# One VectorE program reordered: cross reciprocal in slot 11, gate denominator behind the keys' last part, slots made in slots 5 to 7

## The reference

```python
x = layernorm(x + attention(x, Wq, Wk, Wv))            # 16 query heads of 16, one shared key and value head
x = layernorm(x + cross_attention(x, context, mask))   # 120 context rows, two projections, a mask added
x = layernorm(x + experts(x, Wg, W1, b1, Wo, bo))      # 8 experts, the top 2 of the gate's softmax
```

## Time and profile before

| | |
|---|---|
| median of three runs | 1377.48 us |
| the profiled execution, its own time | 1376.5 us |
| its span, first to last instruction | 1374.5 us |
| TensorE busy over the span | 1267.1 us (92%) |
| VectorE busy | 1100.1 us (80%) |
| ScalarE busy | 743.4 us (54%) |
| GpSimd busy | 639.8 us (47%) |
| TensorE's granted clock, mean | 0.972 |
| one full step of the first stage | 21.2 us (kstack at 478.29 us and at 499.49 us) |
| draining steps 33 to 38 | from 733 to 805 us |

### The profile page before, as it was taken

How to read it: one execution, slowest core, us unless ns; L and a number is a source line. 1 busy time by engine, 2 the same in 40 slices (tenths; PEclk the granted TensorE clock), 3 DMA queues, 4 the chain that set the end, 5 groups by cost and what they waited for, 6 DMA issues and landing times.

```text
span 1374.5 us, 30245 instructions
## 1 busy us (share of the span) xinstructions
PE 1267.1 (92%) x7734; PEld 895.6 (65%) x7735; DVE 1100.1 (80%) x3115; ACT 743.4 (54%) x1740; POOL 639.8 (47%) x917
## 2 busy tenths in 40 slices
PE   6898999999999999999998659999999999987997
PEld 4444555556556565555654447788888888867997
DVE  0566898898988889989897657788887888876997
ACT  1235777787877788878886313232232322323555
POOL 3011345545554545554554523685555555651333
PEclk9999999999999999999999859999999999998999
DMA  7747588797887978867565775898888888877885
GB/s 187 183 100 143 107 219 202 209 227 189 220 195 189 205 196 216 177 184 162 137 145 187 275 281 89 142 151 134 125 136 133 132 133 128 137 119 233 280 280 178
DMA packets 194871, 242.73 MB, mean 177 GB/s; under 512 B 21712, under 2 KB 144592, under 8 KB 190544
## 3 DMA queue, kind: packets, MB, share of 16 engines
q1 hardware_dynamic: 159392, 153.70, 46.0%
q0 software_dynamic: 26128, 54.94, 23.3%
q10 hardware_dynamic: 9248, 32.86, 7.0%
HBM read 142.46 MB, written 120.24 MB: 191 GB/s over the span
## 4 chain that ended last, share of the span: by engine, by line
PE 70%; DVE 10%; DMA 8%; issue 6%; SPq 2%; POOL 2%; ACT 1%; ACTq 0%; POOLq 0%; DVEq 0%
PE psHb L1441 7%; PE psHb L1438 7%; PE psHb L1437 7%; PE psS L729 5%; PE psO L644 5%; PE psHa L1438 5%; PE psHa L1437 5%; PE psHa L1441 5%; PE psB L673 4%; PE psT L739 4%; DVE negmax L1070 4%; DMA qstack<-q_parts 3%; PE psX L1461 2%; PE psHa L1494 2%; DMA xt<-in_x_t 2%
## 5 line engine op out<-in xcount | busy, mean ns | idle before, releaser
L1070 DVE TENSOR_REDUCE negmax<-psS 128x2 f32<-128x512 f32 x512 | 346.7, 684 | 85.8 <-PE psS L729 84.7
L904 ACT ACTIVATE probs<-psT 128x512 f32<-128x512 f32 x512 | 299.6, 599 | 139.8 <-PE psT L739 127.1
L1518 ACT ACTIVATE hb<-hb 128x512 f32<-128x512 f32 x135 | 85.4, 632 | 285.9 <-DVE hb L1593 248.3
L1402 POOL DMA_INDIRECT g_rows<-g,slot x135 | 212.9, 1577 | 35.9 <-issue 32.9
L729 PE MATMUL psS<-kstack,qstack 96*128 96x256 bf16 x1024 | 194.7, 272 | 31.1 <-DMA qstack<-q_parts 12.6
L739 PE MATMUL psT<-qstack,kstack 99*128 99x512 bf16 x512 | 193.6, 381 | 4.6 <-ACT probs L904 4.4
L729 PEld LDWEIGHTS psS<-kstack,qstack 96*128 96x128 bf16 x1024 | 89.9, 101 | 102.7 <-DVE negmax L1070 30.8
L503 POOL DMA_INDIRECT lists<-x,slots x128 | 128.4, 1003 | 33.9 <-issue 30.1
L644 PE MATMUL psO<-probs,vaug 128*32 128x512 f32 x1024 | 138.8, 615 | 0.4 <-ACT probs L904 0.4
L1602 DVE SCALAR_TENSOR_TENSOR g<-g,xe,hb 128x512 f32<-128x512 f32 x135 | 101.6, 752 | 24.8 <-ACT hb L1518 11.3
L1593 DVE TENSOR_TENSOR hb<-psHb,b 128x512 f32<-128x512 f32 x135 | 93.2, 690 | 31.1 <-issue 27.8
(11 more groups left out here) (210 smaller groups left out, 2792.2 us busy)
## 6 DMA issues: line engine op xcount, KB each, us to landing
qstack<-q_parts SPq DMA_DIRECT2D x192, 128.0 KB
g_rows<-zero_rows ACTq DMA_DIRECT2D x20, 1024.0 KB, 6.6
xe<-lists SPq DMA_DIRECT2D x135, 132.5 KB
rows<-g_rows SPq DMA_DIRECT2D x32, 512.0 KB, 4.5
q_parts<-qpart SPq DMA_DIRECT2D x32, 384.0 KB
sums<-x SPq DMA_DIRECT2D x32, 264.0 KB
x2in<-sums SPq DMA_DIRECT2D x32, 264.0 KB, 3.4
xt<-in_x_t SPq DMA_DIRECT2D x32, 256.0 KB
```

Source lines behind the costliest of these rows:

```text
L904: nc.scalar.activation(probs[:, u % PT, :], psT[:, u % 2, :], ACT.Exp, scale=SELF_SCALE).then_inc(sm["exp_done"], 1)
L1070: v.tensor_reduce(negmax[:, b1.s2, 2 * hp:2 * hp + 2, c], psS[:, u % 2, :].rearrange("p (h k) -> p h k", h=2), AX.X, ALU.max, negate=True) ...
L1402: pool.indirect_dma_start(out=dram["g_rows"], out_offset=bass.IndirectOffsetOnAxis(ap=slot[:, o.s8:o.s8 + 1], axis=0), in_=g[:, o.s8], in_ ...
```

## The change

The instructions are the same; their places in the in-order programs differ.

- chosen, slotf and slots of batch b7 move from slots 0, 1, 2 to slots 5, 6, 7 of the same step.
- GpSimd no longer waits for slots_ready between the two parts of the queries; it waits ahead of the first dispatch, in every step.
- crec moves from slot 13 to slot 11.
- The gate's denominator moves: its first operation from slot 12 to slot 14, behind the keys' last part; its second from slot 13 to slot 15; its reciprocal from slot 14 to behind slot 15, ahead of L1192, which needs it.

```diff
--- before.py
+++ after.py
@@ -518,7 +518,6 @@
                 pool.tensor_tensor(qpart[:, t.s2, 1], qrest[:, t.s2], one_c[:, :].unsqueeze(2).to_broadcast([P, DC, S]),
                                    ALU.mult).then_inc(sm["q_split"], 1)
 
-                wait(pool, "slots_ready", done(b7))
                 wait(pool, "q_split", 2 * t.n + 1)
                 pool.tensor_tensor(qpart[:, t.s2, 2], qrest[:, t.s2], qpart[:, t.s2, 1], ALU.subtract
                                    ).then_inc(sm["q_split"], 1)
@@ -526,8 +525,7 @@
                 expert_constants()
             if active(b7):
 
-                if not active(t):
-                    wait(pool, "slots_ready", done(b7))
+                wait(pool, "slots_ready", done(b7))
                 dispatch(b7, 0)
             if active(b4):
                 wait(pool, "att_normed", done(b4, 2))
@@ -1073,19 +1071,19 @@
                 if u == 0 and active(b6):
                     wait(dve, "y2_ready", done(b6))
                     stats(y2, stats2, b6, "stats2_ready")
-                if u == 0 and active(b7):
+                if u == 5 and active(b7):
                     wait(dve, "slot_link", 3 * b7.n + 1)
                     v.tensor_tensor(chosen[:, b7.s2], hot[:, b7.s2],
                                     place[:, b7.s2].unsqueeze(2).to_broadcast([P, QC, 2, E]), ALU.mult
                                     ).then_inc(sm["slot_link"], 1)
                 if u == 1 and active(b6):
                     moments(stats2, mv2, b6, "var2_ready")
-                if u == 1 and active(b7):
+                if u == 6 and active(b7):
                     wait(dve, "slot_link", 3 * b7.n + 2)
                     v.tensor_reduce(slotf[:, b7.s2], chosen[:, b7.s2], AX.X, ALU.add).then_inc(sm["slot_link"], 1)
                 if 1 <= u <= 4 and active(b2):
                     split_max(b2, u - 1)
-                if u == 2 and active(b7):
+                if u == 7 and active(b7):
                     wait(dve, "slot_link", 3 * b7.n + 3)
                     v.tensor_copy(slots[:, b7.s2], slotf[:, b7.s2].rearrange("p c k -> p (c k)")
                                   ).then_inc(sm["slots_ready"], 1)
@@ -1147,14 +1145,9 @@
                 if u == 12 and active(b4) and not draining(t):
                     wait(dve, "y1_ready", done(b4))
                     stats(y1, stats1, b4, "stats1_ready")
-                if u == 12 and active(b6):
-
-                    wait(dve, "gate_exp", done(b6))
-                    v.scalar_tensor_tensor(gden[:, b6.s2], gsum[:, b6.s2], GATE_EPS, gtop[:, b6.s2, :, 0], ALU.mult,
-                                           ALU.add).then_inc(sm["gate_link"], 1)
                 if u == 13 and active(b4) and not draining(t):
                     moments(stats1, mv1, b4, "var1_ready")
-                if u == 13 and active(b6):
+                if u == 15 and active(b6):
                     gate(5)
                     v.tensor_tensor(gden[:, b6.s2], gden[:, b6.s2], gtop[:, b6.s2, :, 1], ALU.add
                                     ).then_inc(sm["gate_link"], 1)
@@ -1162,12 +1155,14 @@
                     wait(dve, "k_mid", done(t))
                     v.tensor_tensor(kstack[64:80, t.s4], krest[64:80, t.s2], ksmall[64:80, t.s2], ALU.subtract
                                     ).then_inc(sm["k_split"], 1)
-                if u == 13 and active(b5):
+                if u == 11 and active(b5):
                     wait(dve, "cross_exp", done(b5))
                     v.reciprocal(crec[:, b5.s2], csum[:, b5.s2]).then_inc(sm["crec_ready"], 1)
                 if u == 14 and active(b6):
-                    gate(6)
-                    v.reciprocal(gden[:, b6.s2], gden[:, b6.s2]).then_inc(sm["gate_link"], 1)
+
+                    wait(dve, "gate_exp", done(b6))
+                    v.scalar_tensor_tensor(gden[:, b6.s2], gsum[:, b6.s2], GATE_EPS, gtop[:, b6.s2, :, 0], ALU.mult,
+                                           ALU.add).then_inc(sm["gate_link"], 1)
                 if u == 14 and active(b5):
                     wait(dve, "crec_ready", done(b5))
                     wait(dve, "cross_out", done(b5))
@@ -1186,6 +1181,8 @@
                 copy_keybias(g, part)
             if active(b6):
 
+                gate(6)
+                v.reciprocal(gden[:, b6.s2], gden[:, b6.s2]).then_inc(sm["gate_link"], 1)
                 gate(7)
                 wait(dve, "hot_ready", done(b6))
                 for c in range(QC):
```

## The result

The changed kernel takes 1383.93 us in the median of 13 runs (1378.82 to 1389.15), the kernel before 1377.48 us on the same chip: ratio 1.0048, interval 1.0033 to 1.0063. The profiled execution spans 1380.4 us, 5.9 us more than before's.

| stretch | before | after | |
|---|---|---|---|
| start to the maxima of step 9, slot 0 | 220.49 | 219.60 | -0.9 |
| 23 full steps, from there to step 32, slot 0 | 493.87 | 491.57 | -2.3 |
| to the last slots | 90.54 | 100.44 | +9.9 |
| from there to the experts' first transposes | 14.58 | 13.18 | -1.4 |
| the experts | 555.07 | 555.63 | +0.6 |

The account below looks back on a forecast made before the run. Bound by TensorE-VectorE handoffs in full steps and a chain of waits in draining steps. 0 + 1.7 + 0.5 + 5.8 = 8.0 us slower, 1385.5 us against the median; 8-in-10 range 1377 to 1393 us.

Parts of the forecast that it names:

- Slot 14, taken at 0: Full steps: moving the gate's denominator and crec brings no earlier kstack; 0 us a step, bounds 0 and -0.15.
- second rival: Full steps: VectorE, not TensorE, sets slot 14, so 19 of 24 steps start 0.15 us sooner; 1382.5 us, chance 0.1.
- The tail, 0.4 us: Behind slot 15 of a full step: linked gate operations ahead of L1192 make base 0.4 us later.
- price of 0.07 us a step: Queries' projection waiting for the later base: 0.07 us in each of 25 steps, bounds 0 and 0.25; 1.7 us.
- The dispatches, "I take +0.1" in "5 of 24 steps": Full steps: later dispatches among qstack's loads cost 0.1 us where the load comes last; 0.5 us in all.
- the forecast's own sign of being wrong: Full steps: qstack's load coming last in most steps, where 4 to 6 of 19 were expected.
- first rival: Full steps: the moved dispatches hold up the loads of qstack, 11 us in place of 0.5; 1396 us, chance 0.15.
- "The loss ends in slot 8, where VectorE waits over 1 us for TensorE": Full steps: the 0.25 us that chosen, slotf and slots add in slots 5 to 7 is absorbed by slot 8's wait.
- The draining steps, 5.8 us: Steps 33 to 38: 1.9 us for 33 and 34, 3.6 for 35, 0.3 for 36 to 38; bounds 3 to 8.
- The stall for y1: Step 33, slot 8: VectorE's statistics wait 2.65 us for GpSimd's y1; costs 1.9 us with step 34.
- step 35: Draining step where GpSimd's queue is the path: y1 waits for slots behind x2t; 3.6 us.
- third rival: Draining steps: their delay doesn't arrive at the experts, or y1 is ready in time; 2.2 us left, 1379.5 us, chance 0.1.

Follow-up runs that it names:

- gate_only: Kernel before with only the gate's denominator and crec moved; chosen, slotf, slots and GpSimd's waits as before: 1380.0 us, ratio 1.0022.
- drain_slots_early: Changed kernel with chosen, slotf and slots back in slots 0 to 2 in draining steps only: 1374.77 us, ratio 0.9982.
- drain_y1_first: Changed kernel with GpSimd adding y1 ahead of its first two dispatches in draining steps: 1377.53 us, ratio 1.0016.
- slots_only: Kernel before with only chosen, slotf, slots and GpSimd's waits moved; gate and crec in their old places: 1379.65 us, ratio 1.0028.
- dispatch_late_again: Kernel before with GpSimd's first two dispatches of a full step held until slot 7's maxima are reduced, third series: 1367.99 us, ratio 0.9978.
- before_again: Kernel before itself, unchanged, profiled once more on the third series' chip: 1369.57 us, ratio 0.9979.
- dispatch_later: Kernel before with GpSimd's first two dispatches of a full step held until slot 8's maxima are reduced: 1376.3 us, ratio 1.001.
- best: Changed kernel with gate and crec in old places, chosen, slotf, slots in slots 0 to 2 in draining steps: 1371.04 us, ratio 1.0035.

## Why the prediction was right in sum and wrong in its parts

**Right in sign and size**: 8.0 us forecast, 6.5 measured, within the range. That is two errors that cancel, and on the chip of the third series, where one of them is missing, the same change costs 0.8%.

**Slot 14, taken at 0: right.** gate_only shows no earlier kstack, so the second rival (VectorE sets slot 14) is out.

**The tail, 0.4 us: right; its price of 0.07 us a step was too low.** Alone it is 0.13 us in the median step, which would be 3.3 us over 25 steps; the sum over 23 steps grew by 1.2. In the two pairs of before and after the weights are only 0.04 to 0.09 us late in the median. On the first series' chip it is more: drain_slots_early and drain_y1_first, which have the new tail, took 491.29 and 492.10 us for steps 9 to 32, slots_only with the old one 488.57, and their weights come 0.16 to 0.18 us later. So the price lies between 1 and 3.5 us here, inside the stated bounds. The Trainium skill's "VectorE: DVE Perf Modes" (The DRAIN you can't avoid) has a semaphore between two operations cost nothing extra, measured there on a row of copies; the runs here have 0.18 to 0.20 us from start to start of linked ones, and 0.04 to 0.11 of unlinked.

**The dispatches, "I take +0.1" in "5 of 24 steps": this step failed.** Its ground was that the bytes ahead of the last load are the same. The load lands 0.4 us later within the step (20.74 to 21.14; third series 0.26) and becomes the last in 17 of 23. That is the forecast's own sign of being wrong, the load last in most steps. Equal bytes are no argument: the same packets of q0 take 9.4% instead of 7.1. That share alone doesn't make a load late, though; in dispatch_late_again it is 8.4% and the load lands early. The first rival, which had this, was right on its mechanism and had 0.15; its price, 11 us, is twice the 5.1 us that steps 9 to 32 grew by on the third series' chip. The rule beside it, of the Trainium skill's "DMA: Bandwidth & Descriptors" (Queues, rings and completion order), that an engine goes round between its queue rows by packets, agrees in sign with both pairs of before and after, but of the 0.75 us that it would have the loads lose, 0.4 and 0.26 us arrive. One point stays open: held to slot 7 on GpSimd alone the dispatches start at 10.62 us and the load lands at 20.64, earlier than before's 20.83; with the changed order they start at 11.06 and it lands at 21.09. The last series shows the late landing with VectorE unmoved, with dispatches at 12.1 us on a chip of the other kind, so a late start seems enough for it. Why 0.4 us of start should matter so much wasn't settled.

**"The loss ends in slot 8, where VectorE waits over 1 us for TensorE": the row was read as slack.** It was a late handoff, 0.69 us where others take 0.04, and on this kind of chip kstack's end comes 0.2 us sooner in the step when the dispatch leaves it (21.12 to 20.95 us in slots_only). That hid the loads' cost; with no late handoff at all (before_again) it comes 0.4 us sooner.

**The draining steps, 5.8 us: mechanism right, size short.** The stall for y1 (2.65 forecast, 2.56 measured) and step 35 (3.6 and 4.0) are as worked out. What was missing for certain is step 37's wait for the dispatches' landing, 1.2 us of the 1.8 there (13.43 against 12.22 where slots came early). A fall of the clock in step 34 comes on top in the first profile of after (20.27 us), but unchanged drains have falls there too (18.68 us in before_again, 18.85 and 18.48 in steps 33 and 34 of dispatch_later, whose drain is before's), and the second profile of after is no longer than those (18.48). That the stall makes the clock fall isn't shown. The cost measured is 11.4 us against undisturbed steps, and 9.9 against the profile of before. The forecast also let all of it arrive at the experts; 1.4 us did not.

**The third rival** (the drain's delay doesn't arrive) is refuted by drain_slots_early: with the drain undone, the cost is gone. In its own terms too: VectorE does wait for y1 in slot 8, and 9.9 less 1.4 us of the drain reach the experts.

**No version beats the kernel before.** drain_slots_early is level on a chip of the first kind; on one of the second, best, which has the same drain and the shorter tail, is 0.35% slower. dispatch_late_again's ratio of 0.9978 is the one that identical code made on its chip (0.9979).

## What to carry to other kernels

A wait that is far longer than the handoff it names is a question, not slack: compare the consumer's start with the producer's recorded end before calling it cover. Equal bytes don't mean equal time: when a transfer moves beside another one, compare the queue's share of busy time for the same packets. In a drain, ask of every step moved back what stands behind it in each queue, down to the buffer that a DMA still reads. And profile the kernel before more than once: its own draining steps 33 and 34 took 35.8 us in one trace and 37.4 in another, nearly as much apart as the whole cost forecast for them.

## What the runs showed of the chip

Two kinds of chip, as far as these traces tell, each chip seen in one series alone. On some (the first pair, the first and the last series) results of TensorE that end beside GpSimd's indirect DMA are signalled 0.1 to 0.85 us late; on others (second and third series) never. A full step of the unchanged kernel is 21.2 us on the one and 20.8 to 20.9 on the other. In before, the late signals of slot 8 come within 0.11 us of the end of the second dispatch; in after and in dispatch_later those of slot 10 come 1.6 and 0.7 us behind its start. What holds them isn't in the trace.

Four indirect DMAs in a row landed 7 us after the last one was issued.

TensorE's clock can differ between executions of one kernel at the same place: in step 34 of the kernel before it is at full speed in one profile and at half, 1.2 GHz, for 3.4 us in the other.
